# A perceiver block: one constants transfer, dummy multiplications moved ahead of the ninth context chunk, the second pair's later order of turns, and the last half-row stored in two parts

## The reference

```python
x = x + matmul(fake_quant(layernorm(x)), fake_quant(ctx))       # ctx: 16 x 1024 x 1024, codes 0..255
x = x + attention(layernorm(x))    # qkv_w 1024 x 3072, 32 heads of 32, rope, causal softmax, out_w, biases
x = x + ffn(layernorm(x))          # W 1024 x 1024 + bias, plus 16 adapters of rank 16, weighted and summed
```

## Time and profile before

| | us |
|---|---|
| median of 3 runs | 632.2 (630.05, 632.2, 635.8) |
| the profiled execution, by the same clock as the runs | 631.85 |
| its span in the trace | 630.2 |
| TensorE busy | 603.4 (96%) |
| VectorE busy | 465.3 (74%) |
| ScalarE busy | 298.0 (47%) |

### The profile page before, as it was taken

The page is one execution under the profiler, slowest core; times in us unless marked ns, Lnnn a source line. Parts: engine busy times, 40 slices in busy tenths (PEclk is TensorE's granted clock), DMA queues, the critical chain, the costliest instruction groups (busy, mean ns, idle before and its releaser), DMA issues.

```text
span 630.2 us, 12824 instructions
## 1 busy us (share of the span) xinstructions
PE 603.4 (96%) x4914; PEld 306.8 (49%) x4914; DVE 465.3 (74%) x923; ACT 298.0 (47%) x376; POOL 10.5 (2%) x19
## 2 busy tenths in 40 slices
PE   3699989989999999999999999999999999999997
PEld 1364444445545545554445455545545554454453
DVE  6599998777768865977577768768874779867661
ACT  5977785864555536453644563555431243210010
POOL 3000000000000000000000000000000000000000
PEclk9899999999999999999999999999999999999999
DMA  8998994861365165317712581364231043222211
GB/s 320 385 387 322 392 372 171 287 216 68 128 220 187 69 222 195 117 67 266 214 73 105 207 266 67 131 223 146 100 122 46 1 144 125 85 94 107 93 75 50
DMA packets 39151, 108.14 MB, mean 172 GB/s; under 512 B 4042, under 2 KB 4298, under 8 KB 39120
## 3 DMA queue, kind: packets, MB, share of 16 engines
q1 hardware_dynamic: 37600, 104.35, 46.5%
q0 software_dynamic: 1088, 3.18, 1.5%
q10 hardware_dynamic: 432, 0.18, 0.1%
HBM read 99.30 MB, written 8.39 MB: 171 GB/s over the span
## 4 chain that ended last, share of the span: by engine, by line
PE 79%; DVE 10%; DMA 5%; issue 3%; ACT 2%; DVEq 0%; ACTq 0%; SPq 0%
PE dense L1169 15%; PE dense L1171 14%; PE dense L1170 14%; PE cross L1207 7%; PE turn L1160 6%; PE dense L1312 4%; PE dense L1314 4%; PE dense L1313 4%; DMA raw<-in_ctx 3%; DVE wq L811 3%; PE score L1275 2%; PE score L1299 2%; DMA wo<-in_ctx 2%; ACT code L344 2%; PE dense L1328 2%
## 5 line engine op out<-in xcount | busy, mean ns | idle before, releaser
L1169 PE MATMUL dense<-wq,xn_h 128*128 128x512 f16 x400 | 151.9, 380 | 0.0
L1170 PE MATMUL dense<-wq,xn_h 128*128 128x512 f16 x400 | 151.6, 379 | 0.0
L1171 PE MATMUL dense<-wq,xn_l 128*128 128x512 f16 x400 | 151.6, 379 | 0.0
L344 ACT ACTIVATE code<-raw,cst,qc 128x1024 uint8<-128x1024 f32 x72 | 87.7, 1236 | 12.4 <-DMA raw<-in_ctx 12.2
L1207 PE MATMUL cross<-code,q1t 128*128 128x512 f16 x256 | 73.8, 390 | 6.9 <-DVE xa L818 4.0
L1171 PEld LDWEIGHTS dense<-wq,xn_l 128*128 128x128 f16 x400 | 39.1, 98 | 47.2
L344 ACT ACTIVATE code<-lnt,cst,qc 128x1024 uint8<-128x1024 f32 x32 | 39.7, 1240 | 44.6 <-DMA lnt<-in_ctx 29.5
L1169 PEld LDWEIGHTS dense<-wq,xn_h 128*128 128x128 f16 x400 | 39.1, 98 | 41.1 <-issue 2.0
L1170 PEld LDWEIGHTS dense<-wq,xn_h 128*128 128x128 f16 x400 | 39.2, 98 | 37.4
L857 DVE SCALAR_TENSOR_TENSOR at<-c,score 128x512 f32<-128x512 f16 x24 | 16.4, 683 | 42.2 <-PE score L1275 42.2
L1207 PEld LDWEIGHTS cross<-code,q1t 128*128 128x128 f16 x256 | 23.8, 99 | 39.3 <-issue 7.5
(11 more groups left out here) (182 smaller groups left out, 965.2 us busy)
## 6 DMA issues: line engine op xcount, KB each, us to landing
raw<-in_ctx SPq DMA_DIRECT2D x72, 512.0 KB, 4.7
lnt<-in_ctx SPq DMA_DIRECT2D x32, 512.0 KB, 4.5
wo<-in_ctx SPq DMA_DIRECT2D x16, 512.0 KB, 9.1
wo<-in_qkv_w SPq DMA_DIRECT2D x12, 512.0 KB, 12.2
wq<-in_qkv_w SPq DMA_DIRECT2D x8, 512.0 KB, 11.8
x_scratch<-xa SPq DMA_DIRECT2D x8, 512.0 KB, 3.0
wq<-x_scratch SPq DMA_DIRECT2D x8, 512.0 KB, 3.6
wq<-in_ctx SPq DMA_DIRECT2D x7, 512.0 KB, 11.7
```

Of the source, the lines that this page charges most:

```text
L344: act.activation(low_bytes, src, ACT.Identity, scale=qc[:, 1:2], bias=z2).then_inc(s_u8, 1)
L1169: pe.matmul(bank[:, :], a_h[:, k, :], w_hi, start=(k == 0 and not started), stop=False)
L1170: pe.matmul(bank[:, :], a_h[:, k, :], w_lo, start=False, stop=False)
L1171: ins = pe.matmul(bank[:, :], a_l[:, k, :], w_hi, start=False, stop=(k == KC - 1 and not last))
```

## The change

It has four parts. (1) The three constants transfers become one of 356 fp32 columns, and VectorE's first instructions wait for all of it. (2) `constants(3)` after chunks 0 to 6 and `constants(16)` after chunk 7 replace `constants(4)` after chunks 8 to 14; `cross_evac(0, 0)` goes ahead of `x_shift(1)`. (3) Pair 1's `qkv` steps 3 to 5 get the table of the later pairs, and `weight_lo(29)` goes behind `softmax_out(1, 1)`. (4) The last column half of pair 7 is computed as two quarters, the first in bank `dense1`, the second in `score0`, each evacuated and stored by itself.

```diff
-        c16 = sb("c16", [P, H_END], F16)
+        c16 = cst[:, C_HALF:C_END].bitcast(F16)
...
-            act.dma_start(cst[:, C_SCAL:C_END], scal).then_inc(s_scal, 16)
-            act.dma_start(c16[:, :], consts16).then_inc(s_c16, 16)
-            act.dma_start(cst[:, 0:C_SCAL], consts).then_inc(s_cst, 16)
+            act.dma_start(cst[:, :], consts).then_inc(s_cst, 16)
...
-            for s in range(2):
-                store(PAIRS - 2 + s, s)
+            store(PAIRS - 2, 0)
+            sp.wait_ge(s_res, 2 * PAIRS - 1)
+            sp.dma_start(out_pair[PAIRS - 1, :, 0:NT], yo[1][:, 0:NT]).then_inc(s_end[1], 16)
+            for n in range(2):
+                sp.wait_ge(s_lastres, n + 1)
+                cols = slice(NT + n * NT // 2, NT + (n + 1) * NT // 2)
+                sp.dma_start(out_pair[PAIRS - 1, :, cols], yo[1][:, cols]).then_inc(s_end[1], 16)
...
-                w(29)
                 softmax_in(i, 0)
                 rotate(i, 2)
                 softmax_in(i, 1)
                 softmax_out(i, 0)
                 softmax_out(i, 1)
+                w(29)
                 rotate(i, 3)
...
-            dve.wait_ge(s_scal, 16)
+            dve.wait_ge(s_cst, 16)
...
+            cross_evac(0, 0)
             x_shift(1)
-            cross_evac(0, 0)
...
+            def y_evac_last():
+                for n in range(2):
+                    dve.wait_ge(s_lastq, n + 1)
+                    cols = slice(NT + n * NT // 2, NT + (n + 1) * NT // 2)
+                    dve.scalar_tensor_tensor(yo[1][:, cols], (D[1], S[0])[n][:, 0:NT // 2], 1.0 / (XSC * WSC), yo[1][:, cols],
+                                             ALU.mult, ALU.add).then_inc(s_lastres, 1)
...
-                    qkv(i, 3, {1: [at(c, 7)], 5: [at(turned, i, 0), at(qk_turn, i, 2)], 6: [at(turned, i, 2), at(p_turn, i, 0)], 7: [at(p_turn, i, 1)]})
-                    qkv(i, 4, {4: [at(evacuated, i, 1), at(qk_turn, i, 3)], 6: [at(c, 8)], 7: [at(c, 9)]})
-                    second_scores = {0: [at(scores, i, 1)]}
...
+                qkv(i, 3, {1: [at(c, 7)], 2: [at(m, 2)], 6: [at(turned, i, 0), at(qk_turn, i, 2)]})
+                qkv(i, 4, {1: [at(turned, i, 2), at(p_turn, i, 0), at(m, 3)], 3: [at(p_turn, i, 1)], 5: [at(evacuated, i, 1), at(qk_turn, i, 3)], 6: [at(scores, i, 1)], 7: [at(c, 8, 9)]})
...
-            for n in range(4):
+            for n in range(CHUNKS):
                 chunk(0, n)
-            for n in range(4, CHUNKS):
-                chunk(0, n)
-                if 8 <= n < CHUNKS - 1:
-                    constants(4)
+                if n < KC:
+                    constants(16 if n == KC - 1 else 3)
...
+            def ffn_last(t):
+
+                pe.wait_ge(s_res, 2 * t)
+                for n in range(2):
+                    bank = (D[1], S[0])[n][:, 0:NT // 2]
+                    for k in range(KC):
+                        w_hi, w_lo = [w[:, k, NT + n * NT // 2:NT + (n + 1) * NT // 2] for w in (wf_h, wf_l)]
+                        pe.matmul(bank, yn_h[1][:, k, :], w_hi, start=(k == 0), stop=False)
+                        pe.matmul(bank, yn_h[1][:, k, :], w_lo, start=False, stop=False)
+                        ins = pe.matmul(bank, yn_l[1][:, k, :], w_hi, start=False, stop=(k == KC - 1))
+                    ins.then_inc(s_lastq, 1)
```

More of the change, by code:

```diff
@@ L47, with build @@
 AX = mybir.AxisListType
-C_ID, C_COS, C_SIN, C_SCAL, C_END = 0, 128, 160, 192, 196
+C_ID, C_COS, C_SIN, C_SCAL, C_HALF, C_END = 0, 128, 160, 192, 196, 356
 H_ID, H_SEL, H_MASK, H_END = 0, 128, 256, 320
-def build(nc, x, ctx_in, consts, consts16, scal, qkv_w, out_w, bias_rows, out_bias, ffn_wt, ffn_bias, lora_a, lora_b, lora_w, out):
+def build(nc, x, ctx_in, consts, qkv_w, out_w, bias_rows, out_bias, ffn_wt, ffn_bias, lora_a, lora_b, lora_w, out):
     x_pair = x.rearrange("(i b) t d -> i (b t) d", b=2)
@@ L151, in build @@
         X = [XX[:, n * NT:(n + 1) * NT] for n in range(2)]
-        s_scal = sem("s_scal")
         s_cst = sem("s_cst")
-        s_c16 = sem("s_c16")
         s_ones = sem("s_ones")
@@ L229, in build @@
         s_res = sem("s_res")
+        s_lastq = sem("s_lastq")
+        s_lastres = sem("s_lastres")
         s_end = [sem(f"s_end{n}") for n in range(2)]
@@ L690, in _ @@
                     store(2 * j + s, s)
+            store(PAIRS - 2, 0)
[5 more added lines that the diff above has]
+                sp.dma_start(out_pair[PAIRS - 1, :, cols], yo[1][:, cols]).then_inc(s_end[1], 16)
             for s in range(2):
-                store(PAIRS - 2 + s, s)
-            for s in range(2):
-                sp.wait_ge(s_end[s], 32 * (PAIRS // 2))
+                sp.wait_ge(s_end[s], 32 * (PAIRS // 2) + 16 * s)
         @block.gpsimd
@@ L1143, in two @@
                         apply3(t + 2, s)
-                    y_evac(t, s, 1)
+                    if last and s:
+                        y_evac_last()
+                    else:
+                        y_evac(t, s, 1)
                     if not last:
@@ L1420, in bias_to_rows @@
             def bias_to_rows():
-                pe.wait_ge(s_cst, 16)
                 pe.wait_ge(s_orow, 16)
@@ L1495, in next_pair @@
                     qkv(i, 2, {0: [at(c, 2)], 1: [at(c, 3)], 2: [at(c, 4)], 3: [at(codes_turned, 1), at(qk_turn, i, 1)], 4: [at(c, 5), at(m, 1)], 6: [at(scores, i, 0)], 7: [at(c, 6)]})
-                    qkv(i, 3, {1: [at(c, 7)], 2: [at(m, 2)], 6: [at(turned, i, 0), at(qk_turn, i, 2)]})
-                    qkv(i, 4, {1: [at(turned, i, 2), at(p_turn, i, 0), at(m, 3)], 3: [at(p_turn, i, 1)], 5: [at(evacuated, i, 1), at(qk_turn, i, 3)], 6: [at(scores, i, 1)], 7: [at(c, 8, 9)]})
-                    second_scores = {}
-                qkv(i, 5, {**second_scores, 1: [at(c, 10, 11), at(m, 4)], 2: [at(c, 12, 13), at(m, 5)], 3: [at(c, 14, 15), at(values_due, i, 0)], 4: [at(values, i, 0)],
+                qkv(i, 3, {1: [at(c, 7)], 2: [at(m, 2)], 6: [at(turned, i, 0), at(qk_turn, i, 2)]})
+                qkv(i, 4, {1: [at(turned, i, 2), at(p_turn, i, 0), at(m, 3)], 3: [at(p_turn, i, 1)], 5: [at(evacuated, i, 1), at(qk_turn, i, 3)], 6: [at(scores, i, 1)], 7: [at(c, 8, 9)]})
+                qkv(i, 5, {1: [at(c, 10, 11), at(m, 4)], 2: [at(c, 12, 13), at(m, 5)], 3: [at(c, 14, 15), at(values_due, i, 0)], 4: [at(values, i, 0)],
                            6: [at(evacuated, i, 0), at(p_turn, i, 2)], 7: [at(p_turn, i, 3)]})
@@ L1509, in next_pair @@
                 project(i, 1, 1)
-            pe.wait_ge(s_c16, 16)
+            pe.wait_ge(s_cst, 16)
             bias_to_rows()
@@ L1559, in two @@
                         y_turn(t + 1)
-                    ffn(t, s, 1, first and s == 0)
+                    if last and s:
+                        ffn_last(t)
+                    else:
+                        ffn(t, s, 1, first and s == 0)
             two(0, True, False)
@@ L1596 @@
         "ctx": f(a["ctx_4096"]),
-        "consts": _constants(),
-        "consts16": _constants16(),
-        "scal": f(np.broadcast_to(scal, (P, 4))),
+        "consts": f(np.concatenate([_constants(), np.broadcast_to(scal, (P, 4)), _constants16().view(np.float32)], axis=1)),
         "qkv_w": f(a["L0_attn_qkv_w"]),
```

## The result

| | before | changed |
|---|---|---|
| median of all paired runs, us | 630.97 (627.57 to 635.8, 16 runs) | 626.63 (626.22 to 629.1, 16 runs) |
| profiled execution / its span, us | 631.85 / 630.2 | 626.48 / 624.8 |

The ratio is 0.9936, 95% interval [0.9916, 0.9956]. The forecast was 628.3 us, a range of 626.0 to 632.2, and 0.88 for a change within 1%: the time lies in the range, 1.7 us under the forecast, and the change is within 1%. The ratio, time changed over time before, is worth 4.0 us of 631, between 2.8 and 5.3 by its interval; in the two profiled spans 5.4 us went. 3.55 had been forecast.

What follows compares the result with a forecast made beforehand. TensorE, busy 603.4 of 630.2 us, was taken as the bound, with idle time mainly in the opening and tail. Opening 1.25, pair 1 1.9 and tail 0.4 sum to 3.55 us off 631.85: 628.3 us, range 626.0 to 632.2.

Steps and rivals of the forecast that it cites:

- One transfer, 0.9 us late: Opening: the single constants transfer lands at 5.95 us, so VectorE starts 0.9 us late and ScalarE 0.6 us late.
- Chunk 7 ends at 23, chunk 8 at 25.1 to 25.7: Opening: products between first chunks run at the low clock, so chunk 8 starts no earlier than the 25.13 before.
- Seven groups leave the path, ScalarE is next, last addition at 30.65: Opening: removed products free 3.0 us; ScalarE and loads bound next, so line 828 starts at 30.65, gaining 1.7 us.
- Tile 5 keeps 0.45 of it; 1.25 us arrive: End of opening: weight tile 5 lands no earlier than 38.31, ahead of `x_high`, so the stage moves by only 1.25 us.
- Pair 1's table, 1.9 us: Pair 1: nine matmuls of necessary work fill TensorE's 2.14 us wait for the key turn's copy; 1.9 us gained, 0.2 left.
- Later pairs: Pairs 2 to 6: new TensorE waits there were named as a sign that the forecast was wrong.
- Rival (c): Pairs 1, 2, 3, 5 and 6 each get pair 4's 0.72 us wait: 631.9 us, no visible gain; chance 0.09.
- Tail, 0.4 us: Last column half: 0.28 us from shorter evacuation, 0.1 from the smaller store; bounds 0.7 gained to 0.2 lost.
- rival (e): Tail: the 24 additional weight loads are exposed, 2.35 us, giving 630.7 us; chance 0.02.
- Rival (d): Opening: TensorE's clock stays low throughout, `x_turn` comes 9 us late, giving 638.6 us; chance 0.03.
- Rival (a): Opening: the loads bound it, so nothing arrives from moving products and reordering: 629.5 us; chance 0.18.
- Rival (b): Opening, pair 1 and tail gain more than forecast, 1.8 + 2.1 + 0.7 = 4.6 us, giving 627.2 us; chance 0.14.

Runs made afterwards that it cites:

- c1: The changed kernel itself, run again beside another set of executions: 626.37 us, ratio 0.9929 to the kernel before.
- u4: Changed kernel with the last column half computed, evacuated and stored whole again: 627.76 us, ratio 0.9946 to the kernel before.
- u1: Changed kernel with the constants in three transfers again, VectorE waiting for the scalars alone: 627.54 us, ratio 0.9941 to the kernel before.
- k2: Changed kernel with no dummy products between the chunks (the 74 behind them stay): 626.32 us, ratio 0.9913 to the kernel before.
- u2: Changed kernel with the dummy products back behind chunks 8 to 14 and none ahead: 629.17 us, ratio 0.9969 to the kernel before.
- k1: Changed kernel with four dummy products behind each of chunks 8 to 14 as well: 628.63 us, ratio 0.9954 to the kernel before.
- n1: Changed kernel with the high part of pair 0's rows ahead of `weight_hi(5)`: 626.59 us, ratio 0.9934 to the kernel before.
- c2: Kernel before with only the dummy products moved as in the change: 630.24 us, ratio 0.9999 to the kernel before.
- b1: Kernel before with sixteen dummy products added behind chunk 7, nothing removed: 631.26 us, ratio 0.9987 to the kernel before.
- u3: Changed kernel with pair 1's old table and `weight_lo(29)` at its old place: 629.26 us, ratio 0.9966 to the kernel before.
- c3: Kernel before with only pair 1's new table and the new place of `weight_lo(29)`: 629.25 us, ratio 0.9961 to the kernel before.
- t1: Changed kernel with pair 1's `weight_lo(29)` back ahead of the softmax, new table kept: 626.87 us, ratio 0.991 to the kernel before.

## Why the prediction was right, and by how much each step

1. **One transfer, 0.9 us late.** Mis-sized: VectorE started 0.34 us late (5.37); the nine traces with the one transfer have 5.03 (c1) to 5.94 (u4), the middle one 5.60, so the 0.9 was the late end of a spread. The step had no bearing: u1 at 4.87 and u4 at 5.94 have the last addition at the same time, 30.37 and 30.38.
2. **Chunk 7 ends at 23, chunk 8 at 25.1 to 25.7.** Missed in the changed kernel's trace, by a misread row: I took the twelve matmuls in 4.04 us for all at the low level, and they are a mixture, 0.34 us each where the low level takes 0.43. In the change the groups of three take 0.69 us up to 17.23 and 0.41 from 18.24 on, so chunk 7 ended at 21.6, its sixteen products ran at the high level, and chunk 8 came at 24.70. But when the level rises is a draw too: in u4, with the same products, it rose at 21.4, chunk 7 ended at 23.6 and chunk 8 came at 26.48. In neither did it move the last addition (30.44, 30.38), so this step had no bearing either.
3. **Seven groups leave the path, ScalarE is next, last addition at 30.65.** Right: 30.44, with TensorE waiting 0.56 and 1.04 us for the codes of chunks 13 and 14. k2 shows that the removal is enough, and against u2 that it is worth some 3 us where the clock mostly falls. The forecast's price for the seven groups took in the low clock of before without saying that it depends on it: with the clock up (k1, u2) they cost the last addition 0.2 to 0.3 us.
4. **Tile 5 keeps 0.45 of it; 1.25 us arrive.** Mis-sized: tile 5 came 0.32 us sooner, at 37.99, and 1.71 us arrived. The step that failed is "it lands no earlier". n1 shows that hardly anything is lost to it. In the traces this gain reached `x_turn(1)` in full (106.05 to 103.75, of which 0.4 is pair 0's, one wait for a chunk's code that is gone). Whether every kernel keeps it isn't settled: c2 and b1 have it in their traces and, by their ratios, no gain; b1's trace gives 1.0 us back in the pairs, c2's keeps it, and u3, with the same old order in pair 1, gains 0.34%.
5. **Pair 1's table, 1.9 us.** Right in mechanism, and in size by the ratios (u3 0.3%, c3 0.4% of 631: 1.9 and 2.5 us, intervals wide); between the two profiled executions `x_turn(1)` to `x_turn(2)` went from 58.19 to 56.64 us, 1.55, and it is 55.95 without a wait (c1). The wait left was 0.48, forecast 0.2: ScalarE began chunk 13 31.1 us behind `x_turn(1)`, 30.8 before. What was missed is that the old order's wait is no number but a spread, 0.59 (u3) to 2.69 us (b1), by when chunk 13's load lands. In the new order the same wait was 0 to 1.4 us in the ten traces that have it (n1 the longest), so it takes off the long end.
6. **Later pairs.** Rival (c) fell: no new waits, and pair 4's 0.72 went. But t1 and n1 have waits of 1.4 to 1.7 us in one pair with the very same table of those pairs, so this was a draw, and not the change's doing as far as one trace can tell.
7. **Tail, 0.4 us.** 0.6 in the ledger: 0.70 from the start of the last VectorE operation on, 0.13 given back by 48 narrower matmuls. The 0.3 us behind the landing were in no term. The earlier trace rows gives 2.0 to 2.1 us for all stores; those are the stores from 600 us on, and over all of them the longest took 3.1. The two last ones in the timeline, and the group of the weight loads of line 1569 there (busy, mean ns):

```profile
621.53 0.27 PE L1568 MATMUL score<-wq,q1t 128*128 128x256 f16 x1
621.64 0.27 PE L1569 MATMUL score<-wq,q1t 128*128 128x256 f16 x1
```

```profile
L1569 PEld LDWEIGHTS score<-wq,q1t 128*128 128x128 f16 x8 | 0.8, 98 | 0.1
```

   They start 0.11 us apart, the time that 256 columns take at 2.4 GHz, with a load of 0.098 us for each: the loads are hidden, and rival (e) fell. The Trainium skill (TensorE: Matmul & The Clock Gate, The mechanism) says in one sentence that a load overlaps matmuls in flight only where the row groups differ; this trace disagrees with that, with full-array loads throughout. The same section also lets a load be pulled ahead that goes to a background weight buffer; the trace is in keeping with this, though it doesn't show where a load goes.
8. **Rival (d)** fell: the clock was up from 18 us on. Rival (a) fell with the 1.71 us that arrived. Rival (b), 627.2, was nearer than the forecast to the 626.63 measured, and mostly by its terms: the opening at 1.71 of its 1.8, the tail at 0.6 of its 0.7; but pair 1 gave 1.55 and not 2.1 in the trace, and the 0.9 us of pair 4 and 0.4 of pair 0 were in no case. The total is 1.7 us high, 0.9 of it because the execution that the sum started from stood that far above the median of 16. Its gain of 3.55 us is near the 4.0 of the ratio and far from the 5.4 of the two traces, of which 0.9 is pair 4's draw; that it came so near the ratio, with the opening 0.5 us too small and pair 1 0.35 too large, is in part luck.

**What stays open.** Where k1's executions lose 1.5 us of span against the changed kernel at the same clock, and why c2's ratio shows no gain. The reorder of `cross_evac(0, 0)` has no kernel of its own: c2 lacks it and has its last addition at 30.58, so the traces show no need of it, but what it is worth to the time isn't measured. And the spread itself: of 89 executions of the kernel before, the 53 with a mean clock of 0.996 or more have a median of 630.2 us, the 36 below 633.6 (the 13 of them at 0.994 630.9, as fast as the first sort). b1 suggests what the second sort is (a long wait of pair 1 with a fall of its own, on top of the opening's), but no execution of that sort was profiled, so that isn't shown. Nor is it shown what moves the landing of chunk 13's load from one execution to the next.

## What to carry to other kernels

A wait read from one trace is one draw when a load feeds it; before pricing an order that removes it, ask how far the load's landing moves, since a gain upstream may be partly eaten by that wait (b1's trace), and an order with more necessary work in front of the wait gains both its mean and its spread. Filler work on the path behind a wait is the first thing to take out (u2 against k2), and its price is to be asked at both levels of the clock; filler that keeps the clock up is worth its place only where the time, and not the clock, shows it (k2).

## What was not expected of the hardware

- After a similar wait the clock fell in one execution and not in another: not after 3.55 us (u2, k2) and 2.62 us (c2), but after 4.02 us (before, 0.57), after 3.52 us (c3, 0.76, a microsecond into the next matmuls) and after 2.69 us (b1, 0.68 from 136 to 140 us). The mean granted clock of u2's other executions says that it fell somewhere in ten of twelve.
- The first chunks' matmuls run at the low level, two in 1.01 us from 15.09, while the window from 16 to 20 us shows a granted clock of 1.00. The trace's record of the clock begins only at 17.91 us, and a stretch without a record counts as 1.00. The durations told the level where the record did not: a group of three dummy products, which waits for nothing, takes 0.69 us there and 0.41 later. The record begins with the rise, and this came at 17.9 us here, at 21.4 in u4 and b1.

```profile
15.09 1.01 PE L1220 MATMUL cross<-code,q1t 128*128 128x512 f16 x2 [0.80 <-issue]
16.00:20.00 4.00, 4.00 (x25) 2.59 (x24) 3.58 (x13) 4.00 (x4) 0.00 (x0) 1.00 1.05 388
```

- The landing of a 256 KB store in the third step is a spread: 2.0 to 3.1 us before (the store issued at 545.73), to 3.2 in the changed kernel (issued at 601.83). The last four stores landed within 1.9 to 2.1 us in both.
